# Issuing batch 1's x from ScalarE's DMA queue in a batched low-rank-update product

## What is computed

```python
z1 = einsum('bfi,bir->bfr', x, v) / 512
z  = einsum('bfr,bor->bfo', z1, v) / 16
y  = einsum('bfi,oi->bfo', x, W) + fc_bias + z + cond
out = x + gelu(y)
```

## Time and profile before

| what | us |
|---|---|
| median of 3 runs | 378.2 (377.73 to 378.36) |
| profiled execution, its own time | 378.88 |
| its span in the profile | 377.1 |
| PE busy | 370.7 |
| DVE busy | 297.8 |
| ACT busy | 207.6 |
| TensorE clock granted in the span | 1.00 of full speed |

### The profile page before, as it was taken

One profiled execution on the slowest core, in us unless ns is written; L12 is line 12 of the kernel. 1 busy time (PEld: TensorE's weight loads), 2 busy tenths in 40 slices (PEclk: granted clock), 3 DMA queues, 4 the chain that ended last, 5 costly groups with the idle time before them and its releaser, 6 DMA issues.

```text
span 377.1 us, 7821 instructions
## 1 busy us (share of the span) xinstructions
PE 370.7 (98%) x3129; PEld 313.8 (83%) x3129; DVE 297.8 (79%) x185; ACT 207.6 (55%) x217; POOL 0.4 (0%) x5
## 2 busy tenths in 40 slices
PE   8989999999999999999999999999999999999995
PEld 6768888888888888888888888888888888888884
DVE  7699778977788977878978778887778977788832
ACT  5377445665456565555565546575445665445532
POOL 0000000000000000000000000000000000000000
PEclk9999999999999999999999999999999999999999
DMA  7999998777977778977778877778976778874222
GB/s 242 218 239 358 277 288 263 214 226 229 272 213 238 213 226 229 245 247 236 197 226 240 253 231 234 202 231 240 262 226 221 212 226 244 252 222 141 111 113 111
DMA packets 24796, 85.49 MB, mean 227 GB/s; under 512 B 4832, under 2 KB 5216, under 8 KB 20816
## 3 DMA queue, kind: packets, MB, share of 16 engines
q1 hardware_dynamic: 24496, 84.92, 76.3%
q10 hardware_dynamic: 288, 0.39, 0.3%
HBM read 35.75 MB, written 33.55 MB: 184 GB/s over the span
## 4 chain that ended last, share of the span: by engine, by line
PE 93%; DMA 3%; ACT 1%; SPq 1%; issue 1%; DVE 0%
PE y L495 87%; PE update L588 3%; DMA x_in<-x_t 2%; DMA x_in<-x_first 1%; PE y L479 1%; PE y L487 1%; PE y L483 1%; SPq L194 1%; ACT result L315 0%; ACT w_high L280 0%; DVE result L425 0%; ACT x_high L287 0%; SPq L206 0%; ACT f_parts L263 0%; SPq L204 0%
## 5 line engine op out<-in xcount | busy, mean ns | idle before, releaser
L495 PE MATMUL y<-x_high,w_high 64*128 64x512 f32 x960 | 190.2, 386 | 1.4 <-ACT result L315 1.4
L495 PE MATMUL y<-x_low,w_high 64*128 64x512 f32 x960 | 190.1, 386 | 0.0
L315 ACT ACTIVATE result<-y,bias 128x512 f32<-128x512 f32 x129 | 81.4, 682 | 154.2 <-PE y L495 146.4
L495 PE MATMUL y<-x_high,w_low 64*128 64x512 f32 x960 | 129.1, 386 | 0.0
L425 DVE TENSOR_TENSOR result<-result,x_in 128x1024 f32<-128x1024 f32 (+1 forms) x66 | 78.3, 1187 | 58.3 <-ACT result L315 58.3
L495 PEld LDWEIGHTS y<-x_high,w_high 64*128 64x128 f32 x960 | 93.2, 184 | 17.5 <-issue 1.8
L495 PEld LDWEIGHTS y<-x_low,w_high 64*128 64x128 f32 x960 | 93.2, 184 | 15.6
L495 PEld LDWEIGHTS y<-x_high,w_low 64*128 64x128 f32 x960 | 93.1, 184 | 15.7
L364 DVE SCALAR_TENSOR_TENSOR full_w<-update,base_w 128x2048 f32<-128x2048 f32 (+2 forms) x35 | 73.4, 2097 | 14.2 <-PE update L588 12.9
L360 DVE TENSOR_TENSOR x_low<-x_in,x_high 128x2048 fp32r<-128x2048 f32 (+1 forms) x35 | 73.5, 2100 | 2.1 <-ACT x_high L274 2.1
L360 DVE TENSOR_TENSOR w_low<-full_w,w_high 128x2048 fp32r<-128x2048 f32 (+1 forms) x35 | 73.6, 2102 | 0.3
(11 more groups left out here) (28 smaller groups left out, 31.7 us busy)
## 6 DMA issues: line engine op xcount, KB each, us to landing
out_t<-result SPq DMA_DIRECT2D x63, 512.0 KB, 3.4
x_in<-x_t SPq DMA_DIRECT2D x31, 1024.0 KB, 6.6
f_stack<-f_parts SPq DMA_DIRECT2D x122, 64.0 KB, 5.2
f_stack<-f_parts SPq DMA_DIRECT2D x61, 128.0 KB, 4.9
x_in<-x_first SPq DMA_DIRECT2D x4, 256.0 KB, 4.5
base_w<-w_t SPq DMA_DIRECT2D x3, 256.0 KB, 5.3
f_parts<-factors SPq DMA_DIRECT2D x1, 768.0 KB, 8.2
base_w<-w_t ACTq DMA_DIRECT2D x1, 256.0 KB, 2.7
```

The lines of the kernel that those rows point to most:

```text
L315: nc.scalar.activation(result[j % SLOTS][:, m, cols], y[m][:, cols], ACT.Gelu, bias=bias[:, bass.ds(b * CHUNKS + m, 1)]).then_inc(gelu_rea ...
L495: return nc.tensor.matmul(y[m][:, :], w[rows, c, m * P:(m + 1) * P], x[rows, c, :], start=first, stop=last)
```

## The change

SP no longer issues batch 1's x. ACT does, on its own queue, behind the instruction that makes w_high of batch 0's chunk 1. The transfer, its size, its destination and its semaphore stay the same.

```diff
@@ -212,7 +212,6 @@
 
             sp.wait_ge(f_again_ready, 1)
             stack_factors(sp, 0, 1)
-            load_x(sp, 0, 1)
             sp.dma_start(f_parts[:, 1, 2, :], factors[1]).then_inc(f_loaded[1], 16)
             stack_factors(sp, 0, 2)
             load_x(sp, 0, 2)
@@ -297,6 +296,8 @@
                 act.wait_ge(full_w_ready, CHUNKS * b + c + 1)
                 nc.scalar.activation(w_high[b][:, c, rest:FEATURES], full_w[:, c, rest:FEATURES],
                                      ACT.Copy).then_inc(w_high_ready, 1)
+                if c == 1:
+                    load_x(act, 0, 1)
 
 
             def gelu(t, j, m):
```

## The result

The change makes the kernel slower. Six executions of the changed kernel had a median of 384.04 us (379.86 to 385.38), against 378.35 (377.73 to 378.71) for six of the kernel before: a ratio of 1.013, 95% interval 1.0082 to 1.0179. The forecast was 378.1 us with a range of 377.0 to 379.4, so it missed by 5.9 us, and the range missed too. A ratio compares only the executions within 1.5% of their kernel's fastest, a median takes all of them, so the two need not match. The profiled execution took 384.24 us with a span of 382.4, against 378.88 and 377.1 before.

A forecast was written before the change was run, and what follows sets the result against it. TensorE, busy 98% of the span, was taken to bound the kernel. Against the median of 378.2, wait removed -1.1, stall added +1.0, ACT and SP zero gave -0.1: 378.1 us, range 377.0 to 379.4.

The forecast's parts named there:

- its running ahead: ACT's queue runs ahead of its engine, so x is issued at 8.25 instead of 9.97; otherwise at 8.87.
- it cost ACT nothing: Issuing x makes ACT 0.5 to 0.7 us late to chunk 2's x_high, covered by over 3 us: cost zero.
- the 0.6 us that SP was to gain: SP drops one issue (0.58), so group 1's factors, batch 2's stack and its x start 0.6 earlier; worth zero.
- w_high of batch 1 waited for the full weights: On ACT, batch 1's w_high waits for DVE's full weights at 16.98 + S; the gelus still end before PE needs them.
- the 1.43 us: PE's single wait for ACT before batch 1's half products, 20.75 to 22.18, would be removed: -1.43 in the profile.
- What the earlier x collides with: x now goes ahead of batch 1's second and third stack transfers, which PE needs at 13.34 with 0.8 us of cover.
- the stall S: PE's wait for batch 1's stack at 13.34: taken as 1.0 us, the middle of 0.7 and 1.4, range 0 to 1.4.
- the slower rival: x's tail on a few engines delays the third stack transfer: 379.6 at half the tail, 380.8 at the whole; chance 0.2.
- this stack itself had no such tail: The prediction's argument against the slower rival, whose late engines would delay batch 1's third stack transfer.
- the half-tail case: Slower rival with half of x's 2.3 us tail: S = 2.5, sum +1.4, 379.6 us.
- x's landing: Batch 1's x lands at 14.2, or by about 15.5 with the stack's turns between, before the 15.7 needed.
- -1.1: Gain against the median from removing PE's wait before batch 1's half products, taken between 0.75 and 1.43 us.

The follow-up runs named there:

- act_c2_holds: Kernel before with x on ACT's queue behind chunk 2, SP held until x landed, batch 2's rank update later on PE: 381.98 us, ratio 1.0085.
- update2_late: Kernel before with only batch 2's rank update moved on PE behind the second phase of batch 1's half products: 379.64 us, ratio 1.0026.
- update1_late: Changed kernel with batch 1's rank update moved later on PE, so products cover the stack's landing: 382.82 us, ratio 1.0084.
- act_c1_holds: Changed kernel with SP held until x landed and batch 2's rank update later on PE: 380.79 us, ratio 1.0069.
- fillers_again: Changed kernel with 40 small matmuls on idle data ahead of PE's wait for batch 1's stack, second run: 380.35 us, ratio 1.004.

## Why the prediction was wrong

**What held.** ACT issued x at 8.40, as forecast from its running ahead, and it cost ACT nothing: the issue took 0.35 us, and x_high of chunk 2 began at 8.93, 0.53 behind the start of w_high, as before. SP's side cost nothing, since PE had no idle at batch 2's rank update; but the 0.6 us that SP was to gain did not come: issuing the factors took 1.75 us, batch 2's stack began at 12.14 (11.28 before) and x 2 went at 16.41 (16.34). w_high of batch 1 waited for the full weights, as written, and before batch 1's half products PE no longer idled: the 1.43 us are off the profile. What the earlier x collides with was named in the right place, batch 1's stack at PE's rank update.

**The step that failed** is the stall S. The prediction took 1.0 with 0 and 1.4 as bounds; the first profile of the change has 5.06 us, the second 2.96. Both bounds were worked out from averages: x's bytes by the rate of all 16 engines, less the idle share of all 16. But the stack is landed only when the last engine has done its share, and an engine that is late has its share of x ahead of the stack's. In the first profile the thirteen shares in step account for 2.1 us of the stall, already more than the upper bound, and the three late ones for the other 3.0. The prediction had seen this in before's trace, the tail of x, and made it the slower rival with the sign right, with S from 2.5 to 3.7 and 0.2 of the chance. Its argument against, "this stack itself had no such tail", was no argument: before, no 1 MB transfer stood ahead of the stack. The range was also said to hold most of the half-tail case, though that case's own 379.6 lies outside 379.4. The rival's price holds for the executions that kept the clock (its 379.6 to 380.8 against 379.46 to 380.84), and is too low for the others: the changed kernel's medians are 383.25 and 384.04.

**x's landing**, forecast by 14.2 to 15.5, was 18.2 and in the second profile 16.0. The prediction let x keep its rate. From issue to landing x took 4.9 us behind batch 1's stack with SP held (act_c2_holds); 5.3 and 5.5 with x 2 behind it; 7.17 before and 6.9 in update2_late, with batch 2's copies behind it; 7.6 to 11.3 with the copies beside it. Holding the copies back did not always help: x issued at 8.2 to 8.4 took 6.5, 8.4 and 9.0. Counted from the eighth of x's sixteen increments to the last, the lag was 1.7 to 5.7 us in all nine profiles with batch 2's copies beside or behind x, 0.2 to 1.3 in five of those without, and 3.1 and 3.2 in the other two. So the copies make a long lag more likely, and it does not need them. An early x also meets the start-up: the last loads of it landed up to 10.9 us in before's trace, and with SP held an x issued 2.1 us earlier (8.41 against 10.50) landed only 0.5 earlier (14.9 against 15.4). x's own lateness costs nothing on ACT's side, as PE waited for the stack anyway, but the stack behind it shares it.

**The term that was missing** is TensorE's clock. The prediction priced a stall at its own length. In the first profile the clock was at 0.50 behind it and the next blocks cost 1.7 us more. Over the executions, those with a fallen clock begin 2.0 us above the others (382.82 against 380.84), but they are likely those with the longer stalls as well, so not all of that is the clock. With fillers in the wait, 11 of 13 executions kept the clock instead of 5 of 12, and the median fell by 2.9, with the same doubt. The Trainium skill ("TensorE: Matmul & The Clock Gate", What's actually happening) says that the clock has two levels and that it is activity that releases the throttle. The windows above agree with it: 0.50 behind the idle stretch, and back at 1.00 once PE had worked again.

With the terms of the two profiles the sum is -1.1 + 3.0 + 0 = +1.9 where the clock holds and -1.1 + 5.1 + 1.7 = +5.7 where it falls. The two groups of the repeated change stand at +0.6 to +2.0 and +3.9 to +7.6 against 378.88, so these terms are of the right size in both, and the result is two groups where the prediction had one number.

**What stays open.** Which DMA engines fall behind in an execution, and why, is not known; the trace does not name them, some of it begins in the start-up loads, and the kernel before has it too (one share of x 1.2 us late; 3 of the 32 executions beside the repeated change at a clock of 0.995 or less, 380.88 to 381.33 us). That it is the copies between buffers, not the bytes, that lengthen the lag rests on one profile. The 10.0 us of the third transfer in update1_late, whose DMA order is the change's, are the same lag in size: two shares of x came over 4 us behind the other fourteen.

## What to carry to other kernels

A small transfer that the critical engine will wait for should not be put behind a large one, on whatever queue: price it by the slowest DMA engine's share of the large one, read from the tail of a transfer in the trace, and not by bytes over the mean rate. The tail differs from one execution to the next (from x's eighth increment to its last 0.2 to 5.7 us), so a single trace gives one draw of it and the price is a range. A stall of TensorE of some microseconds is to be priced twice, once for its length and once for the products that may run at half clock behind it. Here a large load that was late was helped by moving what shares the engines with it (x 5.3 us instead of 7.17), and not by an earlier issue.

## What was not expected of the hardware

- A 128 KB transfer issued 1.15 us after a 1 MB one landed 9.3 us after its issue (3.2 without it ahead), and the 1 MB one, issued earlier, landed later: 9.8 us against 7.17.
- One to three of the sixteen shares of a 1 MB transfer came 1.2 to 4.8 us behind the others, in some executions and not in others; in act_c1_holds the last share of x alone was out from 15.48 to 17.34.
- Where shares of x came late, shares of the weights issued at 4.8 us had often been late before it: two and two in update1_late, one and one in fillers_again.
- The length of PE's idle stretch alone did not decide on the clock: it stayed at 1.00 behind 2.96 us in one execution, and was at 0.50 behind 2.90, 2.95, 3.10, 3.77, 3.85, 4.05, 4.91 and 5.06 in others.
